# Maxima of the wide self attentions by row halves of the array behind the values, and a reordered opening, in a four-layer transformer kernel

## What is computed

```python
emb = t @ W + b; scale, shift = jnp.split(emb, 2, axis=-1)      # the "cond" step
h = (x - mu) * rsqrt(var + EPS) * (1.0 + scale) + shift
q, k, v = h @ Wq, h @ Wk, h @ Wv                                # 16 heads x 64
sim = einsum('bihd,bjhd->bhij', q, k) * 0.125                   # 1024 x 1024 per head
attn = softmax(sim, axis=-1)                                    # exp(sim - row maximum) / sum
x = einsum('bhij,bjhd->bihd', attn, v) @ Wo + bo + x
```

## Time and profile before

| | us |
|---|---|
| median of 3 runs | 4756.79 (4752.77 to 4774.43) |
| the profiled execution, its own time | 4768.35 |
| its span (first to last instruction) | 4766.6 |
| busy: PE, PEld | 4157.7 (87%), 2548.7 (53%) |
| busy: DVE, ACT, POOL | 3079.0 (65%), 2080.2 (44%), 1344.8 (28%) |
| mean granted TensorE clock | 0.935 of full speed |

### The profile page before, as it was taken

How to read it: one execution, slowest core, us unless ns; L and a number is a source line. 1 busy time by engine, 2 the same in 40 slices (tenths; PEclk the granted TensorE clock), 3 DMA queues, 4 the chain that set the end, 5 groups by cost and what they waited for, 6 DMA issues and landing times. The chain is left out here.

```text
span 4766.6 us, 56541 instructions
## 1 busy us (share of the span) xinstructions
PE 4157.7 (87%) x20828; PEld 2548.7 (53%) x20828; DVE 3079.0 (65%) x4625; ACT 2080.2 (44%) x3756; POOL 1344.8 (28%) x664
## 2 busy tenths in 40 slices
PE   6899989789998878888888876788799899997989
PEld 4343356633335665554555445567555555545768
DVE  4888855688885655667666763345477777774455
ACT  2555544355554433333333434454244444444541
POOL 1000001200001024554555553321144444451120
PEclk9999989899998988999999998889899999998999
DMA  4223231122323142222222215333223233215420
GB/s 120 29 53 47 42 56 34 45 27 52 45 42 59 32 79 65 46 52 63 56 62 62 50 29 120 80 63 73 62 61 72 54 70 76 63 39 135 104 64 18
DMA packets 158515, 286.64 MB, mean 60 GB/s; under 512 B 36458, under 2 KB 70052, under 8 KB 157216
## 3 DMA queue, kind: packets, MB, share of 16 engines
q1 hardware_dynamic: 158240, 283.03, 28.6%
HBM read 105.01 MB, written 29.64 MB: 28 GB/s over the span
## 5 line engine op out<-in xcount | busy, mean ns | idle before, releaser
L948 PE MATMUL PS<-t 128*128 128x512 f32 (+4 forms) x7896 | 2006.1, 386 | 224.1 <-ACT t L1390 100.9
L948 PEld LDWEIGHTS PS<-t 128*128 128x128 f32 (+2 forms) x7896 | 1258.7, 188 | 786.0 <-issue 259.5
L1390 ACT ACTIVATE t<-PS 128x512 f32<-128x512 f32 (+2 forms) x1600 | 1164.7, 750 | 1094.6 <-PE PS L948 1088.1
L1667 DVE TENSOR_REDUCE t<-PS 128x1 fp32r<-128x1024 f32 x512 | 621.9, 1220 | 311.8 <-PE PS L1020 305.6
L1128 PE MATMUL PS<-t 128*32 128x512 f32 (+2 forms) x4352 | 816.9, 615 | 0.2
L1671 DVE TENSOR_REDUCE t<-PS 128x1 f32<-128x512 f32 x1024 | 649.2, 682 | 75.5 <-PE PS L1024 74.1
L1961 POOL TENSOR_TENSOR t<-t 128x1024 f32<-128x1024 f32 x256 | 621.1, 2426 | 148.1 <-ACT t L1390 123.6
L1024 PE MATMUL PS<-t 96*128 96x512 bf16 x1024 | 374.9, 396 | 37.5 <-DVE t L1671 13.5
L1020 PE MATMUL PS<-t 128*128 128x512 f32 x1024 | 340.4, 416 | 59.2 <-DMA t<-t 26.8
L1957 POOL TENSOR_TENSOR t<-t 128x1024 f32<-128x1024 f32 x64 | 155.6, 2431 | 747.7 <-PE PS L1138 469.7
L1899 POOL TENSOR_TENSOR t<-t 128x2048 f32<-128x2048 f32 x24 | 109.6, 4569 | 899.2 <-DMA t<-in_rows 560.6
(11 more groups left out here) (134 smaller groups left out, 3936.2 us busy)
## 6 DMA issues: line engine op xcount, KB each, us to landing
t<-t SPq DMA_DIRECT2D x512, 128.0 KB, 3.6
t<-t SPq DMA_DIRECT2D x256, 256.0 KB, 3.9
t<-scr_n SPq DMA_DIRECT2D x288, 128.0 KB, 6.3
scr_n<-t SPq DMA_DIRECT2D x72, 256.0 KB, 2.2
t<-t SPq DMA_DIRECT2D x256, 64.0 KB, 2.0
t<-in_L_Wg SPq DMA_DIRECT2D x16, 768.0 KB, 4.5
t<-in_L_W SPq DMA_DIRECT2D x36, 256.0 KB, 3.3
t<-in_L_Wo SPq DMA_DIRECT2D x64, 128.0 KB, 2.6
```

The lines of the kernel that those rows point to most:

```text
L948: ins = e.matmul(out, l, r, start=i == 0, stop=i == len(terms) - 1, tile_position=tp)
L1390: e.activation(dst, src, ACT.Exp, scale=S.L.scale).then_inc(*expd.inc((S.i, i)))
L1667: e.tensor_reduce(S.MT[m % 2][:, qt, j:j + 1], o, AX.X, ALU.max, negate=True).then_inc(*bank_free[k].nth(nth))
```

## The change

1. **Wide maxima.** A step "max" is now (qt, half): two matmuls of 64 rows each, head 0 in rows 0 to 63 and head 1 in rows 64 to 127 of the array (`tile_position=(64 * i, 0)`), high part of q by high part of k, into the two banks of one slot. The DVE reduction takes 128x1024 as 2 x 512 into two columns of a small tile NMX, and "mturn" begins with one more DVE reduction (NMX, 16 to 8 columns, negated). The PE's transposes now wait for that (`max_part`).
2. **Their place.** Two max steps directly behind each group of values instead of one every eighth of a unit; "mturn" at n - 0.3 (ahead of the values of .72) instead of n - 0.27 (behind them).
3. **The opening.** The SP issues the first layer's cond weights ahead of x; cond of L0 comes first, three products of L1's cond behind each of the four turns, those of L2 and L3 go into L0's self attention (L2 between the first projections and the values, L3 between the 32 first maxima), as does the bias of x; the first weights are split ahead of the turns.

```diff
-            out = [("max", S, m, j, qt, 0) for j in range(2) for qt in range(4)]
-            return out + [("mturn", S, m)]
+            return [("max", S, m, 0, qt, half) for qt in range(4) for half in range(2)] + [("mturn", S, m)]
...
-                    u.smq = [[qs[:, j, 0, 128 * t:128 * t + 128] for t in range(4)] for j in range(2)]
-                    u.smk = [[ks[:, j, 0, 512 * h:512 * h + 512] for h in range(2)] for j in range(2)]
+                    u.smq = [[qs[64 * j:64 * j + 64, j, 0, 128 * t:128 * t + 128] for t in range(4)] for j in range(2)]
+                    u.smk = [[ks[64 * j:64 * j + 64, j, 0, 512 * h:512 * h + 512] for h in range(2)] for j in range(2)]
...
-    order.append(("setup",))
-    norm0 = norm_steps(first)
-    order.extend(norm0[:9])
-    order.extend(("cond", L) for L in Ls)
-    order.extend(norm0[9:])
-    order.extend(weight_steps(first))
+    order.append(("setup", 0))
+    order.append(("mod_load", Ls[0]))
+    order.append(("setup", 1))
+    order.append(("w_load", first, 0))
+    order.append(("setup", 2))
+    order.extend(("mod_load", L) for L in Ls[1:])
+    order.extend(("ln_stats", first, t) for t in range(8))
+    order.append(("ln_rstd", first))
+    order.append(("w_split", first, 0, 0))
+    order.append(("cond", Ls[0], 0, 12))
+    order.extend(("ln_norm", first, t) for t in range(4))
+    for q in range(4):
+        order.append(("ln_turn", first, q))
+        order.append(("cond", Ls[1], 3 * q, 3 * q + 3))
+        order.append(("ln_split", first, q))
+        order.extend(("ln_norm", first, t) for t in range(2 * q + 4, min(2 * q + 6, 8)))
...
+                        plan.put(-16, 0, [("cond", Ls[2], 0, 8)])
+                        plan.put(-9, -8, [("cond", Ls[3], 2 * i, 2 * i + 2) for i in range(6)])
+                        plan.put(-7.5, 0, [("ln_bias", first)])
...
-                        plan.put(max(n - 1.5, -0.5), n - 0.5 if n > 1 else 0.6, max_steps(S, n)[:8])
-                        plan.put(n - 0.27 if n > 1 else 0.75, 0, max_steps(S, n)[8:])
+                        maxima = max_steps(S, n)
+                        for i in range(4):
+                            at = n - 1.28 + 0.25 * i if n > 1 else -0.4 + 0.25 * i
+                            plan.put(at, 0, maxima[2 * i:2 * i + 1])
+                            plan.put(at, 0, maxima[2 * i + 1:2 * i + 2])
+                        plan.put(n - 0.3 if n > 1 else 0.6, 0, max_steps(S, n)[8:])
...
-                    for h in range(2):
-                        ins = e.matmul(o[:, 512 * h:512 * h + 512], u.smq[j][qt], u.smk[j][h], start=True, stop=True)
+                    for i in range(2):
+                        ins = e.matmul(o[:, 512 * i:512 * i + 512], u.smq[i][qt], u.smk[i][half], start=True, stop=True,
+                                       tile_position=(64 * i, 0))
...
-                if S.L.style == 64:
-                    for j in range(2):
-                        k, nth = where["max", S.i, m, j, 3]
-                        w.wait_ge(bank_free[k], nth)
-                else:
-                    w.wait_ge(max_part, (S.i, m, "end"))
+                w.wait_ge(max_part, (S.i, m, "end"))
...
-                    if m >= 2:
-                        k, nth = where["turn", S.i, m - 2, 0]
-                        w.wait_ge(bank_full[k], nth)
-                    o, k, nth = full(w, ("max", S.i, m, j, qt))
-                    e.tensor_reduce(S.MT[m % 2][:, qt, j:j + 1], o, AX.X, ALU.max, negate=True
-                                    ).then_inc(*bank_free[k].nth(nth))
+                    if m:
+                        w.wait_ge(max_part, (S.i, m - 1, "end"))
+                    o, k, nth = full(w, ("max", S.i, m, qt, half))
+                    e.tensor_reduce(S.NMX[:, 2 * qt:2 * qt + 2, half:half + 1].rearrange("p j h -> p (j h)"),
+                                    o.rearrange("p (j n) -> p j n", j=2), AX.X, ALU.max).then_inc(*bank_free[k].nth(nth))
...
+                    e.tensor_reduce(S.MT[m % 2][:, :, :].rearrange("p q j -> p (q j)"), S.NMX[:, :, :], AX.X, ALU.max,
+                                    negate=True).then_inc(*max_part.inc((S.i, m, "end")))
```

More of the change, by code:

```diff
@@ L957, in tensor_program @@
                 src = sT if L.silu else cT
-                for m in range(L.nmod):
+                for m in range(lo, hi):
                     o, k, nth = take(w, ring, ("cond", L.i, m))
@@ L1017, in tensor_program @@
                 if S.L.style == 64:
-                    o, k, nth = take(w, ring, ("max", S.i, m, j, qt))
-                    for h in range(2):
-                        ins = e.matmul(o[:, 512 * h:512 * h + 512], u.smq[j][qt], u.smk[j][h], start=True, stop=True)
+                    o, k, nth = take(w, ring, ("max", S.i, m, qt, half))
+                    for i in range(2):
+                        ins = e.matmul(o[:, 512 * i:512 * i + 512], u.smq[i][qt], u.smk[i][half], start=True, stop=True,
+                                       tile_position=(64 * i, 0))
                     ins.then_inc(*bank_full[k].inc(nth))
@@ L1311, in scalar_program @@
             elif what == "cond":
-                L, = a
+                L, lo, hi = a
                 w.wait_ge(setup_in[0], 0)
-                for m in range(L.nmod):
+                for m in range(lo, hi):
                     o, k, nth = full(w, ("cond", L.i, m))
@@ L1325, in scalar_program @@
                     w.wait_ge(ln_split, (p.i, q - 1) if q else (p.i - 1, 3))
-                w.wait_ge(mod_made, "all")
+                w.wait_ge(mod_made, (p.L.i, "all"))
                 o, k, nth = full(w, ("ln", p.i, q))
@@ L1502, in vector_program @@
             if what == "setup":
+                if not a[0]:
+                    e.memset(ones[:, :], 1.0).then_inc(*set_up.inc("ones"))
+                if a[0] < 2:
+                    continue
                 w.wait_ge(setup_in[2], 0)
                 e.tensor_copy(identb[:, :], ident[:, :]).then_inc(*set_up.inc("ident"))
-                e.memset(ones[:, :], 1.0).then_inc(*set_up.inc("ones"))
             elif what == "cond":
-                L, = a
+                L, lo, hi = a
+                if hi < L.nmod:
+                    continue
                 k, nth = where["cond", L.i, L.nmod - 1]
@@ L1520, in vector_program @@
                         if aff is None:
[L1521 removed]
+                            e.tensor_copy(mb, mod[:, 2 * sh + k, :]).then_inc(*mod_made.inc((L.i, "all")))
                         else:
@@ L1705, in vector_program @@
                 S, m = a
+                if S.L.style == 64:
+                    for half in range(2):
+                        k, nth = where["max", S.i, m, 3, half]
+                        w.wait_ge(bank_free[k], nth)
+                    if m >= 2:
+                        k, nth = where["turn", S.i, m - 2, 0]
+                        w.wait_ge(bank_full[k], nth)
+                    e.tensor_reduce(S.MT[m % 2][:, :, :].rearrange("p q j -> p (q j)"), S.NMX[:, :, :], AX.X, ALU.max,
+                                    negate=True).then_inc(*max_part.inc((S.i, m, "end")))
                 rows = 12 if S.L.style == 16 else 2
@@ L1981, in sync_program @@
             if what == "setup":
-                e.dma_start(cols[:, :], A["cols"]).then_inc(*setup_in[0].inc(0, 16))
-                e.dma_start(cT[:, :, :], A["cT"]).then_inc(*setup_in[1].inc(0, 16))
-                e.dma_start(ident[:, :], A["ident"]).then_inc(*setup_in[2].inc(0, 16))
-                e.dma_start(sel[:, :], A["sel"]).then_inc(*setup_in[3].inc(0, 16))
+                part, = a
                 x = A["x"].rearrange("(t p) d -> p t d", p=128)
-                for h in range(4):
-                    e.dma_start(X[:, 4 * h:4 * h + 4, :], x[:, 4 * h:4 * h + 4, :]).then_inc(*x_in[h].inc(0, 16))
-            elif what == "cond":
+                if not part:
+                    e.dma_start(cT[:, :, :], A["cT"]).then_inc(*setup_in[1].inc(0, 16))
+                    e.dma_start(cols[:, :], A["cols"]).then_inc(*setup_in[0].inc(0, 16))
+                elif part == 1:
+                    for h in range(2):
+                        e.dma_start(X[:, 4 * h:4 * h + 4, :], x[:, 4 * h:4 * h + 4, :]).then_inc(*x_in[h].inc(0, 16))
+                    e.dma_start(ident[:, :], A["ident"]).then_inc(*setup_in[2].inc(0, 16))
+                else:
+                    e.dma_start(sel[:, :], A["sel"]).then_inc(*setup_in[3].inc(0, 16))
+                    for h in range(2, 4):
+                        e.dma_start(X[:, 4 * h:4 * h + 4, :], x[:, 4 * h:4 * h + 4, :]).then_inc(*x_in[h].inc(0, 16))
+            elif what == "mod_load":
                 L, = a
```

12 lines of the change are left out of this document (8 added, 4 removed).

## The result

| | us |
|---|---|
| before, 4 runs | 4761.02 (4752.77 to 4774.43) |
| after, 4 runs | **4986.25** (4983.63 to 4993.85) |
| ratio | **1.0473**, 95% interval 1.0445 to 1.0501 |
| the profiled execution, its own time; its span | 4985.66; 4983.9 |
| mean granted TensorE clock | 0.921 of full speed |

Slower by 225 us, where 126 on the profile and 4883 were forecast: the sign was right and so was the place (the wide self attentions), the size was not, and the time lies outside the range. In the new kernel scores are L967, exponentials L1407, values L1143, the spread of the sums L1153, maxima L1039 with reduction L1688, turn L1100 with L1734 ahead of it, projection L1185, norm L1786 and L1788, layer norm L1580, L1591, L1593 on DVE and L988 on PE, POOL's sums of keys L1991.

A forecast was written before the change was run, and what follows sets the result against it. PE's sequence was taken to bound L3's wide self attention, with ACT holding up L2's; 48 + 89 + 19 - 30 = +126 on the profiled 4768.35 gave 4894, or 4883 us against the median, range 4765 to 4975.

The forecast's parts named there:

- Quarters with maxima: Wide self attentions: row-half pairs cost 0.67 us against 0.45 replaced, +0.22 in 192 quarters and +0.1 in 56: +48 us.
- The turn's wait: Wide quarter .47: PE waits about 2.2 us for DVE in 34 bare units, 1.0 in 14 of L3: +89 us.
- The projection's slot: Wide units: the projection waits for the reduction of the first max step ahead, 0.3 us in 62 units: +19 us.
- The opening: Kernel start: first projection at about 41 us instead of 77.33, part given back in L0's attention: net -30 us.
- Layer norm units: Units 10 to 13 and 26 to 29 of each wide layer; the forecast gave them no price of their own.
- the halves do not run side by side: Rival, wide maxima: a quarter's row halves take 1.14 instead of 0.67 us in 248 quarters, +117: 5000 us; chance 0.06.
- PE was the bound: Rival, wide maxima: the halving pays in full, -117 us, plus the opening: 4610 us; chance 0.05.
- covered: Rival: the turn's wait is covered and pairs cost no more than before, leaving only the opening: 4727 us; chance 0.07.
- small losses: Rival: a pair near 0.47 us, the turn waiting about 1.1 in 34 bare units: 4765 us, no measurable change; chance 0.10.

The follow-up runs named there:

- b1: The changed kernel's places (clusters behind the values, turn at n - 0.3), but with the old whole-height maxima, one reduction per head and no merging reduction: 5005.95 us.
- a1: The changed kernel with only the turn of the maxima moved from just ahead of the values of .72 to just behind them: 4892.88 us.
- e1: The changed kernel with halves spread evenly and the turn behind the values in eight of each layer's 32 units (n 11 to 14, 27 to 30): 4924.46 us.

## Why the forecast was right in direction and wrong in size

The runs build the change up step by step: opening alone 4734.5; halves, evenly spread 4827.8 (+93); halves in clusters behind the values, turn behind them 4892.9 (+65); turn ahead of the values 4986.3 (+93).

- **Quarters with maxima** (+48 forecast): right for the plain ones. 5.17 for 5.18 us, 0.66 for 0.67 from maxima to scores, both by the rows of one run before any row with halves existed. What cannot pay is the halving at this place: its 0.28 us a quarter, change of mode included, are less than the 0.47 that leaving ACT's wait costs (b1's 5.44 against 4.97). A single pair takes 0.43 us, where its columns alone would take 0.235. The Trainium skill (TensorEngine Tiling (Array Packing), Key Properties) says that a change of tiling mode drains the array, and the 0.43 us agree; it gives no size.
- **The turn's wait** (+89 forecast, as "DVE needs 4.85 us, PE 3.3"): the sum came out near, 93 by a1, but by luck, out of parts that were off both ways. In the two stages a1 and the change differ by 99 us: 60 in the bare units outside the layer norm units (48 forecast), 35 in the layer norm units (26) and 4 where nat64 fills the quarter (14). Its cause was told incompletely. The step followed DVE's order to L1734 and did not look at which bank the turn writes; that bank comes free only 0.1 us earlier, so the number came out right. The size of a bare wait was a little high (1.80 for 2.2), and the clock, which the forecast named only as an upper bound, more than filled the gap: 37 us in stretched groups of values, where the opening alone has 4.
- **The projection's slot** (+19 forecast): in the list it is L1185 waiting 13.8 us in L3 and 13.0 in L2, 26.8 for 19.
- **The opening** (-30 forecast): -23 to -27. The first projection came 4 us later than worked out: the sum let the 12 products run at their own pace and did not look at ACT's order, where they wait 5.58 us.
- **Layer norm units: the step that failed.** The forecast multiplied bare quarters by their number and gave the layer norm units the same price as the others; of the 156 us that it has for the wide stages, 45 or so fall on them (a quarter of 67, and 12 bare turn quarters at 2.2 us among the 34). They lost 125.6. The other units lost 128.5 for about 111. So some 80 of the 99 us that were missing come from a quarter of the units. Of the 125.6, 91 are in the units with layer norm operations: there DVE's queue holds these ahead of the reductions or of L1734, both slots are taken by one cluster, and PE's own layer norm turn waits for it. The other 34 are in units 12 and 13, 24 of them in L2, where nat64's split stands ahead of L1734; so the name fits most of the loss and not all. e1, which spreads the maxima in these units alone, gets 62 us back.

Of the rivals, "the halves do not run side by side" gave 5000 us, close to the measured time, and is false: 0.66 us for two pairs. A time alone would have seemed to confirm it. "PE was the bound" (4610) and "covered" (4727) are out by the quarters and by a1, and "small losses" (4765, a turn's wait of 1.1 us and a pair near 0.47) by the 1.80 and the 0.66 us.

## What to carry to other kernels

Before placing a step earlier on one engine, write down everything it waits for on every other engine, also the buffer that it writes, and read each from the queue in the busiest unit, not in the plain one: with an engine that works in order, the units where queues meet (here a quarter of them) carried most of the miss. Two steps in a row that fill a ring of two slots stop every other user of the ring until the first of them is consumed; the same steps one by one leave a slot open. And work put where the engine would wait anyway costs less even at full size (a quarter of 4.84 us, against 5.44 behind the values), so halving it there gains next to nothing (4.80).

## What the runs showed of the hardware that I had not expected

DVE's small layer norm operations stretch beside POOL. Groups by line and shape, L3's self attention of the changed kernel, then the same lines in its opening, where POOL does nothing beside them (busy us, mean ns):

```profile
L1593 DVE TENSOR_TENSOR t<-t 128x512 fp32r<-128x512 f32 x8 | 14.7, 1840 | 0.3
L1580 DVE TENSOR_SCALAR t<-t 128x256 f32<-128x256 f32 x16 | 14.6, 924 | 0.0
...
L1580 DVE TENSOR_SCALAR t<-t 128x256 f32<-128x256 f32 x8 | 2.8, 406 | 0.0
L1593 DVE TENSOR_TENSOR t<-t 128x512 fp32r<-128x512 f32 x4 | 2.8, 692 | 0.1
```

In the quarter shown above two L1580 take 5.03 us beside two additions of POOL of 4.88 us together, and not the 0.41 each of the opening: each ends just behind one of POOL's, so it seems to run only when that has ended. The Trainium skill (SBUF — State Buffer, Who interferes with whom) says that the two engines share a port pair, held as a lock for a whole instruction, and that the later one is blocked; these rows agree, though they do not show which of the two came first, and no run here took POOL's additions away to test it. In the kernel with the old maxima the same lines are shorter:

```profile
L1581 DVE TENSOR_SCALAR t<-t 128x256 f32<-128x256 f32 x16 | 11.7, 730 | 0.0
L1594 DVE TENSOR_TENSOR t<-t 128x512 fp32r<-128x512 f32 x8 | 8.7, 1086 | 0.3
```

So a new order on PE also changed which DVE operations meet POOL, for 9 us of DVE's time in these two groups in this layer, in just the units where PE waits for it. How much of the layer norm units' loss that makes stays open.
